# Experts' weights of layers 2 and 3 held in SBUF and copied per tile into a ring by VectorE

## What is computed

```python
scores = softmax(flat @ router_w.T + router_bias)
topk_scores, topk_idx = top_k(scores, 4)                  # 4 of 32 experts per token
h = silu(einsum('nd,ehd->neh', flat, gate_w)) * einsum('nd,ehd->neh', flat, up_w)
expert_out = einsum('neh,edh->ned', h, down_w)
out = (take_along_axis(expert_out, topk_idx) * topk_scores).sum(axis=1)
out = out + silu(flat @ sgate_w.T) * (flat @ sup_w.T) @ sdown_w.T    # shared expert
```

```python
indices = argmax(softmax(x @ Wr + br))                    # 1 of 8 experts per token
for i in range(8):
    mask = (indices == i)[..., None]
    h = relu((x * mask) @ W1[i] + b1[i])
    out = out + (h @ W2[i] + b2[i])
```

## Time and profile before

| what | value |
|---|---|
| device time, median of 3 executions | 2706.49 us |
| the three executions | 2703.36, 2706.49, 2708.31 us |
| span of the profiled execution (its own time) | 2709.2 us |
| instructions | 44319 |
| PE / DVE / ACT / POOL busy, whole span | 2224.6 / 1611.4 / 1261.1 / 752.8 us |
| moved by DMA, whole span | 185.07 MB |

### The profile page before, as it was taken

How to read it: one execution, slowest core, us unless ns; L and a number is a source line. 1 busy time by engine, 2 the same in 40 slices (tenths; PEclk the granted TensorE clock), 3 DMA queues, 4 the chain that set the end, 5 groups by cost and what they waited for, 6 DMA issues and landing times. The chain is left out here.

```text
span 2709.2 us, 44319 instructions
## 1 busy us (share of the span) xinstructions
PE 2224.6 (82%) x15435; PEld 1297.3 (48%) x15454; DVE 1611.4 (59%) x3356; ACT 1261.1 (47%) x1914; POOL 752.8 (28%) x886
## 2 busy tenths in 40 slices
PE   3787787884698998999989689999997987685674
PEld 1455555563244444444444334444444785444374
DVE  6666676752674675756747787777772443654102
ACT  2334444322255666666565245665665442331143
POOL 1335253543010110200200133424231115662432
PEclk8888988887798999999998699999998998895597
DMA  2112200003021020111100011222213992110285
GB/s 65 41 48 56 49 10 2 3 1 106 32 73 30 20 62 20 38 44 38 56 26 20 19 46 57 80 58 74 63 42 121 318 322 72 39 41 14 80 265 178
DMA packets 144400, 185.07 MB, mean 68 GB/s; under 512 B 27153, under 2 KB 118450, under 8 KB 139159
## 3 DMA queue, kind: packets, MB, share of 16 engines
q1 hardware_dynamic: 103391, 136.81, 17.0%
q0 software_dynamic: 13696, 32.02, 3.8%
q10 hardware_dynamic: 27126, 13.75, 1.8%
HBM read 129.75 MB, written 52.21 MB: 67 GB/s over the span
## 5 line engine op out<-in xcount | busy, mean ns | idle before, releaser
L1766 DVE TENSOR_REDUCE a_mpart<-a_mx 128x1 f32<-128x512 f32 (+3 forms) x1216 | 745.7, 657 | 298.0 <-PE a_mx L1500 167.5
L1674 ACT ACTIVATE a_prob<-a_st 128x1024 f32<-128x1024 f32 (+3 forms) x768 | 608.1, 812 | 517.0 <-PE a_st L1533 370.7
L1497 PE MATMUL a_mx<-a_ka,a_qa 96*128 96x512 bf16 (+3 forms) x1536 | 436.1, 342 | 63.7 <-DVE a_mpart L1766 30.0
L1530 PE MATMUL a_st<-a_qa,a_ka 96*128 96x512 bf16 (+3 forms) x1536 | 420.7, 336 | 26.2 <-ACT a_prob L1674 14.5
L1548 PE MATMUL a_acc<-a_prob,a_v_aug 128*9 128x512 f32 (+3 forms) x3072 | 326.1, 501 | 0.0
L1497 PEld LDWEIGHTS a_mx<-a_ka,a_qa 96*128 96x128 bf16 x1536 | 143.0, 100 | 345.3 <-DVE a_mpart L1766 164.5
L1533 PE MATMUL a_st<-w_mask_t,identb 128*128 128x128 bf16 x1024 | 211.8, 226 | 0.0
L1530 PEld LDWEIGHTS a_st<-a_qa,a_ka 96*128 96x128 bf16 x1536 | 147.5, 100 | 127.0 <-ACT a_prob L1674 26.2
L1421 POOL DMA_INDIRECT x_rows<-l_xn,l_slots x128 | 124.9, 976 | 259.1 <-ACT a_prob L1674 248.6
L2190 PE MATMUL t_psu<-t_xsT,t_w 128*128 128x128 f32 x960 | 155.3, 296 | 23.3 <-DMA t_w<-in_l_experts 17.0
L1500 PE MATMUL a_mx<-w_mask_q,identb 128*128 128x128 bf16 x768 | 167.9, 228 | 0.0
(11 more groups left out here) (457 smaller groups left out, 3987.3 us busy)
## 6 DMA issues: line engine op xcount, KB each, us to landing
t_w<-in_l_experts SPq DMA_DIRECT2D x160, 192.0 KB, 4.4
t_w<-in_l_experts SPq DMA_DIRECT2D x40, 514.0 KB
a_qa<-q_parts_dram SPq DMA_DIRECT2D x96, 192.0 KB
a_ka<-k_parts_dram SPq DMA_DIRECT2D x96, 192.0 KB
x_rows<-zeros SPq DMA_DIRECT2D x25, 512.0 KB, 3.6
t_xs<-x_rows ACTq DMA_DIRECT2D x40, 256.0 KB, 5.2
y_rows<-t_y POOLq DMA_DIRECT2D x40, 256.0 KB
q_parts_dram<-a_parts SPq DMA_DIRECT2D x24, 256.0 KB
```

What stands on the lines that cost most here:

```text
L1497: ins = pe.matmul(to, qa[G % NQ][0:QK_PAD, h0 + k, qi * P:(qi + 1) * P], ka[G % NQ][:, h0 + k, lo:hi], start=not masked_first, stop=k == p ...
L1530: ins = pe.matmul(to[:, lo:HALF], ka[G % NQ][:, h, j * P:(j + 1) * P], qa[G % NQ][0:QK_PAD, h, ch * HALF + lo:(ch + 1) * HALF], start=True ...
L1674: act.activation(prob[:, k_at % NP_, 2 * pair:2 * pair + 2, lo:HALF], sring[s % 2][:, :, lo:HALF], ACT.Exp, scale=1.0 if alibi(G // NG) el ...
L1766: dve.tensor_reduce(mpart[:, G % 2, h0:h0 + per, qi, piece], slot[:, 0:per * width].rearrange("p (k w) -> p k w", k=per), X, ALU.max).then ...
```

## The change

`expert_tiles` is replaced by two functions. In layer 2 (`routed_tiles`) SP loads the weights of all 32 experts once into `held` (48 KB per partition), in ten transfers of 1, 1, 2 and then seven times 4 experts. DVE copies the weights of each tile's expert from `held` into the ring `w` of 8 buffers, 6 tiles ahead; it reads the experts' numbers into its own registers (8 at a time), and its tile loop is written out in the program, as is GpSimd's. PE and ACT keep their hardware loops. So that a tile `s` never needs an expert above `s`, the routing (`r_count`) now gives every expert at least one tile.

In layer 3 (`switch_tiles`) the weights of the 8 experts and their base rows go into `l3_held` (8 times 1156 columns), loaded by SP in the stage before (`linear_attention`). DVE copies the 1156 columns of a tile's expert into a ring of 6. The base is added from the ring. The stores of a pair no longer wait for the whole half. All loops are written out; the order within PE and ACT is even, without iterations.

```diff
+        bounds = [0, 1, 2, 4, 8, 12, 16, 20, 24, 28, E2]
+            held = sb(c, n + "held", [P, E2, width])
             w = sb(c, n + "w", [P, body, width])
...
+            def keep_weights(eng, s, chosen):
+                if s in bounds[:-1]:
+                    eng.wait_ge(held_loaded[bounds.index(s)], 16)
+                wait(eng, dn_made, s + 1 - body)
+                e = bass.ds(chosen, 1)
+                eng.tensor_copy(w[:, s % body], held[:, e].rearrange("p e k -> p (e k)")).then_inc(w_kept, 1)
...
                 @block.sync
                 def _(sp):
-                        for k in range(body):
-                            wait(sp, dn_made, it * body + k + 1 - body)
-                            e = bass.ds(chosen[k], 1)
-                            sp.dma_start(w[:, k], weights[e].rearrange("e p k -> p (e k)")).then_inc(w_loaded[k], 16)
...
+                    for k, (lo, hi) in enumerate(zip(bounds, bounds[1:])):
+                        sp.dma_start(held[:, lo:hi], weights[lo:hi].rearrange("e p k -> p e k")).then_inc(held_loaded[k], 16)
...
-                        pe.wait_ge(w_loaded[k], 16 * (it + 1))
+                        pe.wait_ge(w_kept, s + 1)
...
                 @block.vector
                 def _(dve):
...
+                    for s in range(6):
+                        next_weights(s)
+                    for s in range(n_tiles):
+                        it, k = divmod(s, body)
+                        if k == 0 and it:
+                            keep(it - 1, pairs - 1)
+                        dve.wait_ge(sg_ready, s + 1)
+                        wait(dve, dn_made, s - 3)
+                        dve.tensor_tensor(h[:, k % 4], sg[:, k % 4], psu[k % 4][:, P:2 * P], ALU.mult).then_inc(h_ready, 1)
+                        if s + 6 < n_tiles:
+                            next_weights(s + 6)
+                        if k >= lag and (k - lag) % 2 == 1:
+                            room(it, (k - lag) // 2)
+                            keep(it, (k - lag) // 2)
+                        if k == body - 1:
+                            room(it, pairs - 1)
```

Layer 3, VectorE, GpSimd's stores, and the load in the stage before:

```diff
+                    def keep_weights(s):
+                        if s % body == 0:
+                            chosen.extend(nc.values_load_multi_w_load_instructions(
+                                experts[0:1, s:s + body], engines=[mybir.EngineType.DVE],
+                                skip_runtime_bounds_check_because="the routing clamps each tile's expert to 0..E3-1")[1])
+                        if s >= room_w:
+                            dve.wait_ge(dn_made, s + 1 - room_w)
+                            dve.wait_ge(y_out, (s - room_w) // 2 + 1)
+                        e = bass.ds(chosen[s], 1)
+                        dve.tensor_copy(w[:, s % room_w], held[:, e].rearrange("p e k -> p (e k)")).then_inc(w_kept, 1)
...
+                    for p2 in range(n_tiles // 2):
+                        at = 2 * p2
+                        if at % hb == 0 and at + hb < n_tiles:
+                            keep_ids(at // hb + 1)
+                        keep(p2)
+                        for s in range(at + room_w, min(at + room_w + 2, n_tiles)):
+                            keep_weights(s)
...
+                            for j in range(hb):
+                                if j % 2 == 0:
+                                    pool.wait_ge(y_out, it * pairs + half * hb // 2 + j // 2 + 1)
+                                pool.indirect_dma_start(y_rows, bass.IndirectOffsetOnAxis(ids[:, it % 2, half, j:j + 1], 0), y[:, half, j], None,
+                                                        bounds_check=y_rows.shape[0] - 1).then_inc(y_stored[half], 16)
...
+                    for e in range(E3):
+                        sp.dma_start(held[:, e, 0:width], weights[e]).then_inc(held_loaded, 16)
+                        sp.dma_start(held[:, e, width:width + D], bases[e:e + 1].to_broadcast([P, D])).then_inc(held_loaded, 16)
+                    sp.wait_ge(held_loaded, 32 * E3)
```

More of the change, by code:

```diff
@@ L2075, in fetch, with routed_tiles @@
                                 bounds_check=rows.shape[0] - 1).then_inc(arrived, 16)
-    def expert_tiles(n, gated, weights, n_e, body, experts, x_rows, y_rows, bases=None, loads=()):
+    def routed_tiles(experts, x_rows, y_rows, weights, loads):
+        n, body = "t2_", 8
         n_tiles = experts.shape[-1]
@@ L2115, in half_tiles, with choices @@
                 return view[:, at:at + hb] if isinstance(at, int) else view[:, bass.ds(at, hb)]
+            def choices(it, engine):
+                at = it * body
+                return nc.values_load_multi_w_load_instructions(
+                    experts[0:1, at:at + body], engines=[engine],
+                    skip_runtime_bounds_check_because="the routing clamps each tile's expert to 0..E2-1")[1]
+            def keep_weights(eng, s, chosen):
[4 more added lines that the diff above has]
+                eng.tensor_copy(w[:, s % body], held[:, e].rearrange("p e k -> p (e k)")).then_inc(w_kept, 1)
             with nc.Block() as block:
@@ L2252, in steps @@
                             wait(act, up_made, s + 1)
-                            if gated:
-                                wait(act, h_ready, s - 3)
-                                act.activation(sg[:, k % 4], psu[k % 4][:, 0:P], ACT.Silu).then_inc(sg_ready, 1)
-                            else:
-                                wait(act, dn_made, s - 3)
-                                for m in range(CH):
-                                    ins = act.activation(h[:, k % 4, m * P:(m + 1) * P], psu[k % 4][:, m * P:(m + 1) * P], ACT.Relu,
-                                                         bias=w[:, k, HID + m:HID + m + 1])
-                                ins.then_inc(h_ready, 1)
-                            if ahead and bases is not None and k % hb == hb - 1:
-                                act.wait_ge(ids_kept, 2 * it + k // hb + 1)
-                                load(it + 1, k // hb)
+                            wait(act, h_ready, s - 3)
+                            act.activation(sg[:, k % 4], psu[k % 4][:, 0:P], ACT.Silu).then_inc(sg_ready, 1)
                     for half in range(2):
@@ L2280, in room @@
                         if 2 * q % hb == 0:
-                            wait(dve, y_stored[2 * q // hb], it * stores)
-                    def keep_ids(it, half):
-                        wait(dve, y_stored[half], (it - 1) * stores)
-                        dve.wait_ge(x_loaded[half], 16 * (it + 1))
-                        dve.tensor_copy(ids[:, it % 2, half], xs[:, half, :, D]).then_inc(ids_kept, 1)
+                            wait(dve, y_stored[2 * q // hb], it * 16)
                     def keep(it, q):
@@ L2315, in _, with next_weights @@
-                    steps(0, None)
-                    if bases is None:
-                        with dve.Fori(1, iters) as it:
-                            steps(it, it - 1)
-                    else:
-                        for it in range(1, iters):
-                            steps(it, it - 1)
-                    keep(iters - 1, pairs - 1)
+                        dve.tensor_copy(y[:, half, at:at + 2], made_y).then_inc(y_out, 1)
+                    chosen = []
+                    def next_weights(s):
+                        if s % body == 0:
+                            chosen.extend(choices(s // body, mybir.EngineType.DVE))
+                        keep_weights(dve, s, chosen[s])
@@ L2634, in _, with linear_attention @@
                                               ).then_inc(ring_v, 1)
-    def linear_attention(q, beside):
+    def linear_attention(q, beside, held, weights, bases):
         n, xT = f"a3{q.b}_", q.xT
```

236 lines of the change are left out of this document (145 added, 91 removed).

## The result

| | before | after |
|---|---|---|
| device time, median of 4 runs each on one chip | 2704.93 us | 2663.21 us |
| ratio, 95% interval | | 0.9853 (0.9829 to 0.9876) |
| profiled execution, its own time beside its span | 2709.2 us | 2662.26 us, 2660.5 us |
| moved by DMA, whole span | 185.07 MB | 141.02 MB |

The account below looks back on a forecast made before the run. Layer 2's expert stage was taken as DMA-bound with PE close behind, layer 3's as waiting for tokens and base rows. Gains 20 + 37 - 3 + 2.5 = 56.5 us from 2706.5 gave 2650 us, range 2632 to 2686.

Parts of the forecast that it names:

- first case: Whole kernel: DVE keeps PE's pace within 10%; 2650 us, own range 2638 to 2664, chance 0.52.
- term 37 - 3 + 2.5: Layer 3: 37 us gained by the last results, 3 lost to late token loads, 2.5 gained on the final scatters.
- term 20: Layer 2's expert stage: last product at 2226 instead of 2246.0, a gain of 20 us.
- the stage stays DMA-bound until the last group: Layer 2's loading phase: 9.7 MB take 30 us, to 2102, when step 22 needs the last group of experts.
- its test: Layer 2, distance of products in 2110 to 2210: 0.90 us per tile forecast, 0.82 if all hidden, 1.05 and more if slower.
- mutual wait: Layer 2, turn of an iteration: PE and DVE wait for each other, 0.6 us per 8 tiles, giving 7.2 us.
- Sum per tile: Layer 2, DVE's work per tile: product and keep, registers, copy and read add to 0.81 us, equal to PE's floor.
- the price is zero: Stage ahead of layer 3: SP's 16 new transfers, 14 us of DMA, cost nothing since GpSimd's issue pace sets the end.
- Rival 3: Layers 2 and 3: GpSimd's issues and VectorE's copies hold each other up; 2684 us, 2667 if one side does; chance 0.14.
- case 2: Layer 2 all hidden, at PE's floor of 0.82 us per tile, gain 31 us; layer 3 in full; 2636 us, chance 0.13.
- case 4: VectorE's weight copies run at 1.0 ns per column, +0.15 us per tile in layer 2; 2673 us, chance 0.11.
- case 5: Slower than before: DVE bounds layer 2 at 1.28 us per tile, from 1.33 eating layer 3's gain; chance 0.06.

Follow-up runs that it names:

- deeper: continuous with four halves of tokens and of results in layer 2 instead of two; layer 2 stage 145.5 us, median 2638.5 us, ratio 0.9759 to the kernel before.
- continuous: Changed kernel, layer 2's PE and ACT loops written out in one order, last results copy later, edits of read_early and held_in_route; 2644.3 us, ratio 0.9764 to before.
- static_source: Changed kernel with layer 2's copies from fixed column blocks, without expert read or register instructions (expert choice left out); layer 2 stage 163.3 us, median 2659.0 us.
- stores_by_sync: Changed kernel with layer 2's 40 result stores issued by SyncE instead of GpSimd; layer 2 stage 172.9 us, 2661.9 us in one run.
- held_in_route: Changed kernel with the 16 loads of layer 3's weights moved into the routing stage; scatters' stage 52.1 us, median 2664.4 us, ratio 0.9843 to before.
- deeper_late: deeper with the seven weight loads for later stages held back until five iterations' results are out; layer 2 stage 144.6 us, median 2634.5 us, ratio 0.9741 to before.
- read_early: Changed kernel with layer 2's read of the next eight experts moved ahead of an iteration's first product; layer 2 stage 168.6 us, median 2661.8 us.

## Why the prediction was right, and where not

**Direction and range.** Faster, and 2663 lies in 2632 to 2686, at the upper end of the first case's own range (to 2664). The size was 56.5 us; the stages that the change touches gave 42.6. The 13.9 us between them are 11.0 too much for layer 2, 5.3 that stood at zero ahead of layer 3, and 2.4 the other way in layer 3. The way in which the change gains was right; that three wrong sizes stayed inside the range is owed to the width of the range.

**Layer 3, term 37 - 3 + 2.5: right.** From the stage's start to its last result 37.1 us were gained. The loss of 3 for late tokens did not occur. The end gained 1.7 us (the last scatter 3.4 us after the last `keep`, before 5.1) where 2.5 stood. The stage gave 38.9 for 36.5.

**Layer 2, term 20: mis-sized, 9.0.** Last product 166.4 us after the stage's start, forecast 155.1. Of the 11.3 us, 4.0 were lost by product 22 (35.1 us after the start, forecast 31.1), 7.3 on the 138 products behind it.
- *The start and the loading phase.* The first product came 10.1 us after the start, forecast 8.6: the copies for tiles 4 and 5 waited for the group of experts 4 to 7 and began after 9.4. Then the step "the stage stays DMA-bound until the last group" failed, though its sum of bytes was no worse than right: the DMA engines moved more than I had set, 358 to 399 GB/s between 2069 and 2089, against 327. It took no account of the order within them. The last group of experts was issued at 2074.6 and landed 15.8 us later, 26.3 us after the start and 8.8 before product 22 began. Tokens landed in 6.6 us in the middle between 2074 and 2094, in 2.9 over the stage, and PE waited 9.3 us for them in all: 6.3 at the start (before: 4.67) and 3.0 in this phase. One such wait, 2.06 us up to 2084.70, cost more than itself: the granted clock, at its upper level of 2.4 GHz since 2077.8, stood at the lower one, 1.2 GHz, from 2084.6 to 2088.0, and the window over it shows 0.66.

```profile
2084.00:2089.00 5.00, 4.30 (x24) 4.30 (x25) 1.47 (x5) 1.30 (x4) 0.00 (x0) 0.66 1.08 399
```

  TensorE did 24 instructions there in 4.30 us, where in deeper 48 went through in the 5 us from 2086, at a clock of 1.00. deeper, which changed no load of experts, took 5.7 us from this phase against continuous, whose clock was 0.66 from 2088 to 2093.
- *The pace.* This was what the forecast called its test: 0.90 forecast, 1.05 and more for cases 3 to 5, and 0.97 measured, nearly midway. Floor, registers and read were each priced, and 0.6 us per iteration was put on the mutual wait. static_source shows that copies with no register instruction and no read already take 7.16 us per eight tiles, the forecast's whole 7.2 (floor 6.6 and mutual wait 0.6). The registers (0.33) and the read (0.25 where it stood) came on top, 7.73 in all; the 0.15 that the stores cost by stores_by_sync lies somewhere in these and was not told apart. The step that failed is "Sum per tile: 0.21 + 0.08 + 0.28 + 0.17 + 0.07 = 0.81 us, as much as PE's floor": it took what VectorE does besides for covered as long as the sum stays at PE's floor. It isn't covered at the turn, where PE waits for VectorE, then branches, then transposes, and only then gets VectorE its next work. Of the turn I had weighed only that `down` of tiles 6 and 7 comes ahead of the next `up`; the wait ahead of the branch (`room`), worth 0.49 us of the distance between `up`s (2.37 to 1.88) and 0.21 us of eight tiles, I had passed over.
- *Prices.* The copy was right (360 ns for 373). The register instructions cost more than 0.26 us, 0.38, but showed as 0.04 per tile where 0.08 was forecast. The read on VectorE took 0.68 us, 0.56 forecast.

**Ahead of layer 3, "the price is zero": wrong, 5.3 us,** within the bound "if each scatter waited for the loads it would be under 5" but for the last tenths. GpSimd's own pace of issue sets the end only as long as the data of its scatters moves. held_in_route gave the 5.3 back.

**Rival 3, GpSimd against the copies: the mechanism is there, the price was far off.** With the copies in the program, GpSimd's scatters of layer 3 took up to 1517 ns; one row of the kernel before and one of after:

```profile
L2155 POOL DMA_INDIRECT y_rows<-t_y,t_ids x40: 967/972/975, 2580.1 to 2684.7; - x40
```

```profile
L2301 POOL DMA_INDIRECT y_rows<-t_y,t_ids x40: 971/975/1517, 2564.0 to 2635.9; - x40
```

and VectorE's copies in layer 2 up to 644 ns, which stores_by_sync removed. Of the 41 copies that overlap a store in time 19 took over 0.4 us, all of which began 0.29 to 0.45 us after the store and ended 0.16 us after it did; those that began ahead of a store took 0.35 to 0.36. The Trainium skill ("SBUF — State Buffer", "Who interferes with whom") says that the two share a port pair and one waits for the other; this trace and that run agree. But it lengthened 19 of 160 copies, and it cost 2.4 us in layer 2, by the one run of stores_by_sync, not 26, and nothing that shows in layer 3, where PE has no gap.

**The other rivals.** No product at PE's floor (case 2) in this kernel, though deeper_late reached it, 6.29 us for eight tiles against a forecast floor of 6.6 with the loop's cost. No slow copy rate (case 4): 760 ns for 1156 columns and 360 for 384 are 0.52 ns per column. No tile of 1.28 us (case 5). Two sums among the rivals were off without touching the forecast: one side alone of case 3 gives 2658 or 2676, of which the 2667 is the middle, and case 5's 1.33 us per tile loses 39 us in layer 2, not 36.

Still open: why the attention stage varies by 10 us between executions of the same code; and how the 4.0 us of the loading phase divide between tokens, results, turns and the clock, since deeper changed tokens and results together. Loading layer 2's experts in the stage before, which might end that phase, wasn't tried, nor whether that stage's buffers leave room for 48 KB per partition.

## What to carry to other kernels

When two engines with nearly the same load feed each other, a sum per tile of each says little: follow one iteration around its turn and list what each waits for before the branch; instructions added to the one that is late there are felt even where the sum says that they fit (0.33 us for registers and 0.25 for the read, per eight tiles). Bytes over bandwidth tells when the last load lands (here even early), not when the work that it feeds is done, so ask which small load stands behind which large one, on the same core, in other stages too. And when the turn was gone, the next waits were those for the room of the neighbours' buffers (two halves of tokens and results); in the profiles doubling them gave the stage 14.5 us, taking out the loop 8.6 against read_early.

## What the runs showed of the hardware

- GpSimd's scatters of the tokens ran eight ahead of their data: pauses of 2.1 us after every eighth, and of 7.1 us when other loads kept the DMA engines busy.
- The profile puts a read of registers from SBUF down as idle time, in the name of another engine ("[1.00 <-PE t_psd L2177]"). On VectorE it took 0.59 to 0.93 us for eight numbers, and the next copy came that much later; behind two copies of results, in read_early, up to 1.10.
- A copy with a register address had 0.27 us of instructions and 0.38 us in all ahead of it, and cost 0.04: in the trace those for the copy at 2151.83 ran from 2151.45 to 2151.78, beside the copy and the product ahead of it (2151.30 and 2151.58).
- Transfers issued faster than they moved held up the engine that issued them: the first of SyncE's loads of 768 KB took 0.47 us to issue, the sixth 2.73, and what stood behind them on SyncE started late: in stores_by_sync the first stores were issued from 2084.69 on, 20 us after the stage's start.
- A copy on VectorE that began while GpSimd issued a plain store of 0.75 us ended 0.16 us after the store (19 copies of 0.47 to 0.64 us, alone 0.36); one that began first took its 0.35 us.
